# Attention on one Trainium2 core: where the softmax denominators are computed, how they reach the output's layout, and which step splits the maxima

## The reference

```python
q = (x @ Wq.T + bq).reshape(B, N, HEADS, HEAD_DIM).transpose(0, 2, 1, 3)
k = (context @ Wk.T + bk)...          # 16 heads of 32 features
v = (context @ Wv.T + bv)...
attn = jax.nn.softmax(jnp.einsum('bhnd,bhmd->bhnm', q, k) * scale, axis=-1)
out = jnp.einsum('bhnm,bhmd->bhnd', attn, v)
x = _layernorm(x + out @ Wo.T + bo)
```

## Time and profile before

| | |
|---|---|
| median of three runs | 2404.8 us (2404.59 to 2414.53) |
| profiled execution | 2413.89 us, span of its trace 2411.9 us |
| attention stage in the trace | from about 940.4 to 2031.3 us |
| busy in the whole span | PE 2100.0 us (87%), DVE 1572.3 (65%), ACT 888.1 (37%), POOL 410.5 (17%) |

### The profile page before, as it was taken

One profiled execution on the slowest core, in us unless ns is written; L12 is line 12 of the kernel. 1 busy time (PEld: TensorE's weight loads), 2 busy tenths in 40 slices (PEclk: granted clock), 3 DMA queues, 4 the chain that ended last, 5 costly groups with the idle time before them and its releaser, 6 DMA issues. The chain is left out here.

```text
span 2411.9 us, 39202 instructions
## 1 busy us (share of the span) xinstructions
PE 2100.0 (87%) x13356; PEld 1346.7 (56%) x13356; DVE 1572.3 (65%) x3000; ACT 888.1 (37%) x2044; POOL 410.5 (17%) x520
## 2 busy tenths in 40 slices
PE   4799999999999985699898999899899996588766
PEld 3667676767767662455454555555455542577632
DVE  5878787786878673366665656566666663667248
ACT  3335353535435340143443424242425242344200
POOL 1011110101111111221121121121112110323012
PEclk9899999999999987799999999999999998799988
DMA  4222303031322203332333232232323212511357
GB/s 158 72 52 70 92 30 112 9 113 31 98 52 69 72 32 122 85 98 63 97 80 96 59 106 67 90 83 76 80 71 106 58 58 90 181 53 61 120 175 263
DMA packets 123125, 211.06 MB, mean 88 GB/s; under 512 B 23360, under 2 KB 40768, under 8 KB 122944
## 3 DMA queue, kind: packets, MB, share of 16 engines
q1 hardware_dynamic: 113728, 189.69, 25.5%
q0 software_dynamic: 9216, 18.89, 3.4%
HBM read 123.56 MB, written 34.08 MB: 65 GB/s over the span
## 5 line engine op out<-in xcount | busy, mean ns | idle before, releaser
L1470 ACT ACTIVATE a_probs<-a_scores 128x512 f32<-128x512 f32 x512 | 276.7, 600 | 369.7 <-PE a_scores L1640 369.4
L1539 DVE TENSOR_REDUCE a_mx<-a_shared 128x1 f32<-128x512 f32 x512 | 320.8, 682 | 130.1 <-PE a_shared L1624 127.3
L1624 PE MATMUL a_shared<-a_ks,a_qs 96*128 96x512 f32 x512 | 236.5, 464 | 46.9 <-DVE a_mx L1539 25.1
L855 PE MATMUL m_proj<-m_xt_hi,m_win_hi 128*128 128x512 f32 x576 | 242.3, 421 | 38.2 <-DVE m_xt_lo L598 24.8
L856 PE MATMUL m_proj<-m_xt_lo,m_win_hi 128*128 128x512 f32 x576 | 230.9, 401 | 0.0
L857 PE MATMUL m_proj<-m_xt_hi,m_win_lo 128*128 128x512 f32 x576 | 230.5, 400 | 0.0
L997 PE MATMUL m_outp<-m_wout,m_g 128*128 128x512 f32 x512 | 226.1, 600 | 2.7 <-issue 2.7
L1640 PE MATMUL a_scores<-a_qs,a_ks 98*128 98x512 f32 x512 | 210.8, 415 | 2.5 <-ACT a_probs L1470 1.5
L588 DVE SCALAR_TENSOR_TENSOR m_acc<-m_proj,m_cw,m_acc 128x511 f32<-128x511 f32 (+2 forms) x216 | 160.8, 748 | 63.6 <-ACT m_acc L420 57.8
L1624 PEld LDWEIGHTS a_shared<-a_ks,a_qs 96*128 96x128 f32 x512 | 100.5, 197 | 176.0 <-DVE a_mx L1539 76.2
L1338 POOL DMA_DIRECT2D a_ks<-a_qk_hi x192 | 94.6, 500 | 559.4 <-PE a_scores L1640 502.3
(11 more groups left out here) (230 smaller groups left out, 3692.2 us busy)
## 6 DMA issues: line engine op xcount, KB each, us to landing
m_dec<-step_decay SPq DMA_DIRECT2D x64, 256.0 KB, 4.1
a_qs<-a_qk_hi SPq DMA_DIRECT2D x256, 64.0 KB, 2.0
e_x<-x SPq DMA_DIRECT2D x16, 1024.0 KB, 6.3
m_ce<-run_decay SPq DMA_DIRECT2D x128, 112.0 KB, 3.0
a_ks<-a_qk_hi POOLq DMA_DIRECT2D x192, 64.0 KB, 2.2
m_xt_in<-x_t_in SPq DMA_DIRECT2D x8, 1024.0 KB, 7.6
m_x_tok<-x_in SPq DMA_DIRECT2D x8, 1024.0 KB, 5.8
x<-m_x_tok SPq DMA_DIRECT2D x32, 256.0 KB, 2.2
```

Of the source, the lines that this page charges most:

```text
L855: pe.matmul(bank[:, :], wh, xt_hi[:, k, :], start=(k == 0), stop=False)
L1470: act.activation(probs[:, n % 2, h, :], scores[t.score_bank(n, h)][:, :], ACT.Exp, scale=SOFT_SCALE).then_inc(exp_ready, 1)
L1539: dve.tensor_reduce(mx[:, i % 2, j, h:h + 1], bank(what)[:, :], AX.X, ALU.max).then_inc(mx_ready, 1)
L1624: pe.matmul(bank(what)[:, :], qs[0:STACK, t.slot(i), h, j * P:(j + 1) * P], ks[0:STACK, t.slot(i), h, :], start=True, stop=True).then_inc( ...
```

## The change

ACT's exponential of the same `p1` scores, now with the maximum as its bias and with the accumulator as an output, gives the denominator of a query as one number in its own partition (`den`, 128 x 16 for a group). It is a step of its own, `sum`, in the order right behind `st` of the next head, five units ahead like `p1`. It writes its exponentials over the scores in the bank, and it is now this step that releases a `p1` bank (`sum_done`). The scores come out negated, since the scale is folded into wq and bq with its sign, so the maximum is a minimum.

`den_bank`, its 32-column products and both copies by ACT are gone. Once a group DVE takes the reciprocal of 128 x 16 numbers (`recip`), PE spreads them over 32 rows a head by sixteen products of a repeated column with the identity (`inv`), DVE copies that out of a shared bank and multiplies it straight with `o_bank` (`norm`). There are now four shared banks. The split of the maxima by DVE (`split`) is a step of its own at the head of a group's last unit, ahead of that unit's maxima. `av` stands ahead of the projection.

```diff
+    def total(n, h):
+        of(n + LEAD, lambda m: [("sum", m // TT, m % TT, h)])
...
+        if u == TT - 1:
+            of(n + TT, lambda m: [("split", m // TT, 0, 0)])
         for h in range(AG):
             maximum(n, h)
             now(("st", gr, u, h))
+            if h:
+                total(n, h - 1)
...
-        if n >= TT:
-            now(*[("norm", gr - 1, c, 0) for c in ((), (0, 1), (), (2, 3))[u]])
+        total(n, AG - 1)
+        if u == TT - 1:
+            now(("recip", gr, 0, 0))
+        if u == 0 and n:
+            now(("inv", gr - 1, 0, 0))
+        if n:
+            now(av(n - 1))
+        if u == 0 and n:
+            now(("norm", gr - 1, 0, 0))
...
-                    "p1": (mx_ready, AG * UNITS, AG * (TT * i + j) + h + 1),
+                    "p1": (sum_done, AG * UNITS, AG * (TT * i + j) + h + 1),
...
+                elif kind == "sum":
+                    act.wait_ge(mx_ready, t.at(AG * UNITS, AG * (TT * i + j) + h + 1))
...
+                    act.activation(scored[:, :], scored[:, :], ACT.Exp, scale=-1.0, bias=mx[:, i % 2, j, h:h + 1],
+                                   accum_out=den[:, i, j, h:h + 1]).then_inc(sum_done, 1)
...
-                    act.activation(o[:, i, :], o_bank[:, :], ACT.Copy)
-                    act.activation(den[:, :], den_bank[:, :], ACT.Copy).then_inc(o_copied, 1)
...
+                elif kind == "recip":
+                    dve.wait_ge(sum_done, t.at(AG * UNITS, AG * TT * (i + 1)))
+                    dve.reciprocal(inv[:, i], den[:, i]).then_inc(inv_ready, 1)
+                elif kind == "inv":
+                    dve.wait_ge(inv_done, t.at(KT, i + 1))
+                    dve.tensor_copy(inv_rows[:, :], bank(what)[:, :]).then_inc(inv_read, 1)
...
+                    dve.tensor_tensor(o[:, i, :], o_bank[:, :], inv_rows[:, :], ALU.mult).then_inc(o_ready, 1)
...
-                            ins = pe.matmul(den_bank[rows, :], onesf[:, 0:AD], probs[:, n % 2, hh, :],
-                                            start=(j == 0), stop=(j == TT - 1))
...
+                    for n in range(TT):
+                        for hh in range(AG):
+                            ins = pe.matmul(bank(what)[hh * AD:(hh + 1) * AD, n * P:(n + 1) * P],
+                                            inv[:, i, n, hh:hh + 1].to_broadcast([P, AD]), ident[:, :],
+                                            start=True, stop=True)
```

More of the change, by code:

```diff
@@ L1062 @@
 STACKS = 3
-BANKS = 3
+SCORE_BANKS = 3
+SHARED_BANKS = 4
 class Turn:
@@ L1108, in av @@
     def av(n):
-        return [("av", n // TT, n % TT, half) for half in range(2)]
+        return ("av", n // TT, n % TT, 0)
     def of(n, names):
@@ L1149, in attention_order @@
             ahead(*[("x", 2 * (n - 2) + k, 0, 0) for k in range(2)])
-    now(*av(UNITS - 1), ("o", KT - 1, 0, 0))
+    now(("inv", KT - 1, 0, 0), av(UNITS - 1), ("norm", KT - 1, 0, 0))
     ahead(("stack", 2, 0, 0))
[L1152 to L1156, removed]
+    for i in range(TT):
+        ahead(("v", i, 0, 0))
     now(*[("out", t, 0, 0) for t in range(TT)], ("end", 0, 0, 0))
@@ L1188, in shared_uses @@
     for (kind, i, j, h), d in part:
-        if kind in ("p1", "xt", "qk", "v", "neg", "out"):
+        if kind in ("p1", "xt", "qk", "v", "neg", "inv", "out"):
             uses.append(((kind, i, j, h), d + shift))
@@ L1196, in bank_plan @@
     start, steady, last = steps
-    bank_of = {use: n % BANKS for n, (use, d) in enumerate(shared_uses(steady))}
-    if len(bank_of) % BANKS == 1:
-        bank_of[shared_uses(steady)[-1][0]] = 1
+    bank_of = {use: n % SHARED_BANKS for n, (use, d) in enumerate(shared_uses(steady))}
+    assert len(bank_of) % SHARED_BANKS == 0
     before = {}
@@ L1252, in attention_stage @@
         rstd = sb("rstd", [P, 2, TT])
-        scores = [ps(f"scores{n}") for n in range(BANKS)]
-        shared = [ps(f"shared{n}") for n in range(BANKS)]
-        o_bank, den_bank = ps("o_bank"), ps("den_bank")
+        scores = [ps(f"scores{n}") for n in range(SCORE_BANKS)]
+        shared = [ps(f"shared{n}") for n in range(SHARED_BANKS)]
+        o_bank = ps("o_bank")
         def bank(use):
@@ L1453, in step @@
                 elif kind == "qk":
-                    if part == "start" and i == 0 and j == 0:
-                        act.wait_ge(small_in, N_SMALL)
+                    if part == "start" and i == 0:
+                        act.wait_ge(ln_v, 1)
                     act.wait_ge(qk_done[j], t.at(KT, i + 1))
@@ L1470, in step @@
                     act.activation(probs[:, n % 2, h, :], scores[t.score_bank(n, h)][:, :], ACT.Exp,
-                                   scale=SOFT_SCALE).then_inc(exp_ready, 1)
+                                   scale=-1.0).then_inc(exp_ready, 1)
+                elif kind == "sum":
+                    act.wait_ge(mx_ready, t.at(AG * UNITS, AG * (TT * i + j) + h + 1))
+                    if h == 0 and j == 0 and not t.first():
+                        act.wait_ge(inv_ready, t.before().at(KT, i + 1))
+                    scored = bank(("p1", i, j, h))
+                    act.activation(scored[:, :], scored[:, :], ACT.Exp, scale=-1.0, bias=mx[:, i % 2, j, h:h + 1],
+                                   accum_out=den[:, i, j, h:h + 1]).then_inc(sum_done, 1)
                 elif kind == "neg":
@@ L1538, in step @@
                         dve.wait_ge(neg_v, t.at(2 * KT, 2 * i - 2))
[L1539 to L1540 removed]
+                        dve.wait_ge(sum_done, t.at(AG * UNITS, AG * TT * (i - 1)))
+                    dve.tensor_reduce(mx[:, i % 2, j, h:h + 1], bank(what)[:, :], AX.X, ALU.min).then_inc(mx_ready, 1)
+                elif kind == "split":
                     dve.wait_ge(mx_ready, t.at(AG * UNITS, AG * TT * (i + 1)))
```

92 lines of the change are left out of this document (44 added, 48 removed).

## The result

The changed kernel takes 2479.3 us (median of four runs, 2473.1 to 2481.8) against 2408.5 for the kernel before beside it: a ratio of 1.029, 95% interval 1.0255 to 1.032. It is slower, as forecast, but by 71 us where 38 were forecast; the time lies inside the range.

What follows compares the result with a forecast made beforehand. PE was taken to bound the attention stage before, ACT to pace its units after. Seven turns x (0.7 + 4.4) = +36, start +2, last turn 0: +38 us on 2404.8, 2443 us; range 2378 to 2485.

Steps and rivals of the forecast that it cites:

- the term of the clock: Attention stage: clock falls while PE is held in each group, 1.2 or 1.0 us a group, 4.4 us a turn.
- the price of a sum: Denominator sum on ACT: 0.70 us to the next start, bounds 0.61 and 0.88; a head costs ACT 1.19 us.
- ACT's waits at full clock: Steady group: ACT's waits for DVE's maxima, late scores and projections, summed to 3.2 us a group.
- the spreading: Sixteen PE products a group that spread the reciprocals: between 0.88 and 4.8 us, taken as 1.5.
- A steady group at full clock: Attention stage, ACT's work 20.7 us plus waits 3.2: 23.9 to 24.0 us against 23.1, +0.9 us.
- the 0.3 of unit 1: Steady group: unit 1's first scores come about 0.3 us late, as PE has inv and av between the units.
- A turn without the clock: First two groups 0, two steady groups 0.9 us each, turn's end -1.1: +0.7 us a turn.
- Rival C: Slower still: sum 0.75 or more, or spreading 4.8 us, or two clock falls a group; some 2475 us, chance 0.12.
- The start: Start of the attention stage: 20 sums lie beside projections, +2 us.
- The last turn: Units without projection +6.7, last five units -3.5, end -5.5, groups and clock +2: together 0.
- A: Rival: same pace by ACT, but the clock holds at 2.4 GHz; 2410 us, chance 0.19.
- B: Rival: sums cost about 0.61 us and most of the 3.2 us of waits go; 2370 us, chance 0.23.

Runs made afterwards that it cites:

- e7: The changed kernel with two PSUM banks for the exponential's scores and five shared ones, instead of three and four: 2427.9 us.
- e4: The kernel before with only the split of the maxima moved to the head of a group's last unit: 2376.0 us.
- e1: The changed kernel with each p1 product in a group's last unit computed two more times into the same bank: 2461.4 us.

## Why the prediction was right in direction and short in size

The step that failed is the term of the clock: 4.4 us a turn were charged, and 7.9 to 8.1 were paid. The pace by ACT, the price of a sum and ACT's waits at full clock came out near their forecast, and the spreading at its lower bound. The parts in turn:

**The rows of the sum.** The exponential and the sum behind it, two heads of a unit on ACT:

```profile
1652.07 0.59 ACT L1481 ACTIVATE a_probs<-a_scores 128x512 f32<-128x512 f32 x1
1652.55 0.66 ACT L1488 ACTIVATE a_shared<-a_shared,a_mx 128x512 f32<-128x512 f32 x1
1653.12 0.21 ACT L1488 ACTIVATION_READ_ACCUMULATOR a_shared<-a_shared,a_mx 128x1 f32 x1
1653.21 0.60 ACT L1481 ACTIVATE a_probs<-a_scores 128x512 f32<-128x512 f32 x1
```

A sum costs 0.66 us to the next start (1652.55 to 1653.21) where I took 0.70 from the earlier trace rows, a head 1.14 and not 1.19. The Trainium skill (ScalarE: Activation LUTs, section "ACT is a hardware spline evaluator") put it below its row for going to PSUM; the number lies where that has it, but no run here wrote the sums to SBUF, so the reason stays open. ACT's busy time in the stage is 694 us; I had said near 740. Of the 46 between them 20 are the 0.04 of 512 sums; the rest isn't traced to a term.

**Spreading.** The 32 records of a group's `inv` start at 1652.22 and the next product at 1653.12:

```profile
1652.22 1.08 PE L1680 MATMUL a_shared<-a_ident,a_inv 128*32 128x128 f32 x32 [0.67 <-ACT a_shared L1488]
1653.12 1.04 PE L1672 MATMUL a_o_bank<-a_probs,a_v 128*32 128x512 f32 x8
```

0.90 us, next to my lower bound of 0.88 and not the 1.5 taken.

**A steady group at full clock.** Forecast 23.9 to 24.0, measured 23.43. ACT's waits there are 1.45 (forecast 1.3), 0.65 (0.4) and twice 0.44 (0.6), and the 0.3 of unit 1 isn't there: 2.98 against 3.2. With ACT busy 20.45 (20.7) that is the group. The parts are right to some tenths, but the forecast is a small difference: +0.3 us against the 23.1 of before, where it had +0.9.

**A turn without the clock.** Forecast +0.7 us, worked out +0.2. That two groups gave 1.1 us less than I had, and the rest of the turn about 0.5 more, is in part luck, and near the limit of what two traces tell.

**The clock: the term that was mis-sized.** Between the first mark and the last lie seven turns: 970.1 us here, 909.7 before, so +60.4 where 36 were forecast. They have 123 us more at the lower level, 57 us by the price above, 8.1 a turn; I had charged 4.4. The forecast had one fall in each group at 1.0 to 1.2 us. In the third and fourth groups of six turns there are 6.8 us a turn at the lower level and none before: 3.1 us by the price, where 2.4 were charged. A fall there costs 1.6 us, as my 1.7, but five of nine last twice as long and cost 3.0 to 3.2; in the one shown above all of it is ACT's wait for the projection (1.45 us becomes 4.47).

In the first two groups and the turn's end there are 18.2 us at the lower level against 8.0: 4.7 us of time, where 2.0 were charged. This is the larger part of what was missing. I had argued that those groups have their falls already; the second, at full clock all through before, now has 6.4 us at the lower level, though it is only 0.4 us longer (27.6 against 27.2 us), as it gained elsewhere.

Whether a fall also brings on the next, over late sums, isn't shown: the waits behind the slow projection (0.16 and, at the group's end, 0.50 and 0.90) are those of a group that held. The mean of 2.0 us a group lies between the 1.1 charged and the upper end, 2 x 1.7. Rival C's "two falls of the clock a group" comes near it; its other two conditions, a dearer sum and a dearer spreading, were false.

**What stood behind that term.** I had seen that unit 3's projection takes the bank of a head whose sum is late, and had written 1.3 us of ACT's idle time beside it. e7 shows that the bank was worth 51 us of the 71: 7.2 a turn, 5.1 of them clock. By my reading the wait and the falls behind it are in good part one cause, and I summed them as two independent terms with a middle value each.

**The start** took 8 us more (first mark at 1031.72 and 1039.78) where I had 2. From 940 us to that mark the clock stands at the lower level for 70 us against 49, and 20 x 0.46 is 9; but e4 and e7 have 63 there and lose 3 to 5, so this term is settled only roughly. **The last turn** was forecast 0 and is: behind the last mark the two spans differ by less than 1 us. That is luck in part. Up to the stage's end it has 20.6 us at the lower level against 3.8 (8 us by the price, where some 2 were meant), so something else gave about as much; no run takes it apart.

**The rivals.** A (the clock holds) is refuted by the rows above. The rule of the Trainium skill behind it (TensorE: Matmul & The Clock Gate, section "Why this matters for your kernels", which the prediction calls "Rules for kernel authors": avoid long idle gaps) doesn't cover this case, in which the rows above have no wait over 0.91 us and the clock fell even so; that page's other section, "A second HAM failure mode: psum-queue depth-cycling", tells of short idling between groups of matmuls that cycle through PSUM banks, with a clock that goes down and up, and the trace agrees with that, without telling which group falls. B (most of the waits go, and a sum costs 0.61) is false: the waits are 2.98 of 3.2 us. e7 comes nearer, with 2.31 us of them (22.76 less 20.45) and a group under 23.1 us, the mark that B set, but it is slower than before all the same.

## What to carry to other kernels

An edit that hands a bank's release from one engine to a slower step lengthens the hold of that bank; list who takes it next, and shift banks with it (here 3 + 4 against 2 + 5 was 51 us) before judging the edit. Waits of half a microsecond that return head by head can cost more than their sum: in nine of fourteen groups the granted clock fell behind them, and the slowed projection kept the pacing engine idle up to 3 us longer. So price the wait and the clock together, ask for the clock in every group of the loop and not only in the one that was looked at, and carry its range into the forecast's range. And test parts of a change alone: the small one, a split issued ahead of its unit, was worth 32 us where the engine that waits for it is the bound, and nothing where another engine is.

## What the runs showed of the hardware

- The granted clock fell to 1.2 GHz behind three waits of 0.18, 0.49 and 0.90 us for PSUM banks in one group, and stayed at 1.00 behind waits of 0.17, 0.49 and 0.91 us in another. With PE kept busier in that unit (e1) it held in all fourteen such groups; in the steady group of e4, with PE busy without a gap, it was 1.00.
- A us at the lower level cost 0.44 to 0.50 us of time in the steady groups of the changed kernel (23.43, 25.14 and 26.43 us with 0, 3.4 and 6.8 us of it), though ACT and not PE set the pace there.
- ScalarE's exponential with bias and accumulator, from PSUM into the same PSUM bank, takes 0.66 us for 512 columns to the next start and 0.45 for 256 (1342.70 to 1343.15), so by these two rows some 0.24 us of it doesn't depend on the columns (an estimate).
- Sixteen fp32 products of 128 columns into 32 rows each (32 records), four heads side by side, take 0.90 us, nearly as long as the output product behind them, 8 records over 512 columns (0.97, 1653.12 to 1654.09).
